# Attention kernel, first stage: layer norm and q, k, v projections rebuilt with split products, a pipeline of chunks and early loads

## The reference

```
xn = layernorm(x)                                         # over the 256 channels
result = x + attention(xn) * silu(ffn(xn))
# attention(x):
q, k, v = x @ Wq.T + bq, x @ Wk.T + bk, x @ Wv.T + bv      # x is 4096 x 256; 16 heads of 16
x*cos + rotate_half(x)*sin                                # on q and k; rotate_half pairs even and odd channels
scores = q @ k.T / sqrt(16), causal; weights = softmax(scores); out = weights @ v
```

## Time and profile before

| | us |
|---|---|
| median of three runs | 3974.87 (3970.74 to 3975.3) |
| the profiled execution | 3964.55 |
| its span, first to last instruction | 3962.8 |
| TensorE busy | 3379.4 |
| DVE busy | 2420.3 |
| ScalarE busy | 1698.9 |
| GpSimd busy | 668.5 |

### The profile page before, as it was taken

The page is one execution under the profiler, slowest core; times in us unless marked ns, Lnnn a source line. Parts: engine busy times, 40 slices in busy tenths (PEclk is TensorE's granted clock), DMA queues, the critical chain, the costliest instruction groups (busy, mean ns, idle before and its releaser), DMA issues. The chain is left out here.

```text
span 3962.8 us, 77279 instructions
## 1 busy us (share of the span) xinstructions
PE 3379.4 (85%) x32524; PEld 2009.1 (51%) x32524; DVE 2420.3 (61%) x3345; ACT 1698.9 (43%) x3090; POOL 668.5 (17%) x464
## 2 busy tenths in 40 slices
PE   5836999999999999999975899985996899995895
PEld 2412333333444333333344676764775677774784
DVE  4325888778767888767524556553553565562554
ACT  1202666677765777777622332321222332321221
POOL 4410000000000000000002333320222433330221
PEclk9966999999999999999878999997998999998897
DMA  5484000020003000000012000000001000000003
GB/s 169 137 146 96 18 9 10 10 62 17 10 26 86 18 17 10 9 4 7 7 57 85 17 18 18 18 7 28 0 0 34 23 18 12 18 12 28 0 0 127
DMA packets 82083, 137.61 MB, mean 35 GB/s; under 512 B 11024, under 2 KB 41872, under 8 KB 80800
## 3 DMA queue, kind: packets, MB, share of 16 engines
q1 hardware_dynamic: 75376, 122.64, 10.9%
q10 hardware_dynamic: 6400, 10.49, 1.0%
HBM read 90.04 MB, written 42.53 MB: 33 GB/s over the span
## 5 line engine op out<-in xcount | busy, mean ns | idle before, releaser
L509 DVE TENSOR_REDUCE mp<-ps_m 128x2 f32<-128x1024 f32 (+3 forms) x1152 | 1287.3, 1135 | 400.3 <-PE ps_m L557 278.8
L485 ACT ACTIVATE probs<-ps_s 128x512 f32<-128x512 f32 (+3 forms) x2304 | 1166.3, 560 | 632.3 <-PE ps_s L592 339.3
L606 PE MATMUL ps_o<-probs,vst 128*32 128x256 f32 (+3 forms) x9216 | 723.9, 386 | 3.1 <-ACT o_sb L474 2.0
L585 PE MATMUL ps_s<-qst,kst 64*128 64x512 f32 (+3 forms) x2304 | 596.0, 496 | 59.5 <-DMA qst<-mrow 50.8
L557 PE MATMUL ps_m<-kst,qst 64*128 64x512 f32 (+3 forms) x2304 | 487.5, 415 | 74.9 <-DMA qst<-null_rows 62.4
L585 PEld LDWEIGHTS ps_s<-qst,kst 64*128 64x128 f32 x2304 | 235.5, 190 | 524.6 <-ACT probs L485 432.6
L606 PEld LDWEIGHTS ps_o<-probs,vst 128*32 128x32 f32 x9216 | 187.9, 110 | 333.7 <-issue 215.4
L462 POOL TENSOR_TENSOR msplit<-negm,mzero 128x16 fp32r<-128x16 f32 x32 | 7.1, 223 | 1759.9 <-DVE negm L515 1759.9
L557 PEld LDWEIGHTS ps_m<-kst,qst 64*128 64x128 f32 x2304 | 229.8, 192 | 132.8 <-issue 69.0
L1205 DVE SCALAR_TENSOR_TENSOR a_t<-a_BP,a_sc,a_tab 128x256 f32<-128x256 f32 x384 | 166.6, 475 | 188.0 <-ACT a_sq L905 187.4
L884 ACT ACTIVATE a_PT<-a_SU 128x1024 f32<-128x1024 f32 (+1 forms) x128 | 122.5, 1009 | 333.0 <-PE a_SU L1002 333.0
(11 more groups left out here) (160 smaller groups left out, 5176.1 us busy)
## 6 DMA issues: line engine op xcount, KB each, us to landing
a_tab<-in_rope SPq DMA_DIRECT2D x32, 512.0 KB
q_parts<-pparts SPq DMA_DIRECT2D x32, 256.0 KB
k_parts<-pparts SPq DMA_DIRECT2D x32, 256.0 KB
v_aug<-pvsb SPq DMA_DIRECT2D x32, 256.0 KB
qst<-q_parts SPq DMA_DIRECT2D x64, 128.0 KB, 2.7
o_raw<-o_sb SPq DMA_DIRECT2D x32, 256.0 KB, 2.1
X<-in_x SPq DMA_DIRECT2D x8, 512.0 KB, 15.7
kst<-k_parts SPq DMA_DIRECT2D x32, 128.0 KB, 5.7
```

The costliest lines, as they stand in the source:

```text
L485: act.activation(probs[:, s % PR, h, off:C], sslots[n % SR][:, off:C], ACT.Exp, scale=float(D) ** -0.5).then_inc(exp_done, 1)
L509: dve.tensor_reduce(mp[b % 2][:, h:h + 2, cc:cc + 1], slot[:, :, 0:width], AX.X, ALU.max).then_inc(max_read, 1)
L585: last = pe.matmul(sslots[n % SR][:, off:C], kst[g % 2][rows, hp, i * P:(i + 1) * P], qst[q_slot(b)][rows, hp, off:C], start=True, stop=True)
L606: last = pe.matmul(ps_o[32 * h:32 * h + VW, lo:hi], vst[g % 2][:, i, h * VW:(h + 1) * VW], probs[:, s % PR, h, lo:hi], start=(i == 0 and h ...
```

## The change

**Split products.** Weights and normalized x are each split into a rounded part and its rest (`w_h`, `w_l`, `xh`, `xl`), and each projection is three products of such parts (`product3`) instead of one fp32 product. The weights of q and k have their even channels first and their odd channels behind, so that no swapped copy is projected: the rotation takes even times cos less odd times sin, and even times sin plus odd times cos. A group is now all of q or all of k (`u`), with even and odd halves (`s`).

**Pipeline.** Each engine works on several chunks by turns: DVE measures chunk c+3, ACT normalizes chunk c+2, PE transposes chunk c+1 between q's and k's products of chunk c. Tables come chunk by chunk. One of the four low parts of a chunk moves to DVE (`low_last`), three stay on POOL. Each of q and k has one buffer of parts. Normalization moves to ACT.

**Values in SBUF.** V stays in one tile `vall`, with rows of 17 and read 32 wide, filled by ACT; its bias comes from a product with ones. `v_aug` and `vst` are gone.

**Null rows.** They are memsets of the whole kst and qst tiles by POOL instead of DMAs; the ones rows come from a small tile. kst1 is zeroed on POOL ahead of its work on block 2, and SP's loads of group 1 wait for that.

**Early loads.** Blocks 0 to 3 of keys and queries of group 0 are loaded in the projection stage, each one chunk after it was written (`preload`).

The diff, cut: removed lines are left out, since they stand above in the kernel before, and so are declarations and the head of each engine's program.

```diff
-def layer_norm_and_project(nc, ctx0, X, x, w_qkv, b_cols, b_v, cos, sin, ident, k_parts, q_parts, v_aug, ones, nulls):
+def project(nc, X, kst, qst, vall, consts, x, w_qkv, b_cols, b_v, cos, sin, ident, identb, mask_k, mask_q, k_parts, q_parts):
...
+            def preload(c):
+                for u in range(2):
+                    sp.wait_ge(parts_out[u], 16 * 4 * (c + 1))
+                load_k_block(sp, kst[0], k_parts, 0, c, pre_in)
+                load_q_block(sp, qst[c], q_parts, 0, c, pre_in)
...
+            for c in range(NC):
+                if c + 4 < NC:
+                    load_x(c + 4)
+                if c == 0:
+                    sp.wait_ge(qst_null, NPRE)
+                for u in range(2):
+                    if u == 1 and c + 2 < NC:
+                        sp.wait_ge(rope_done, 8 * (c + 1))
+                        load_cs(c + 2)
+                    sp.wait_ge(lo_pool, 3 * c + 2 + u)
+                    if u == 1:
+                        sp.wait_ge(lo_dve, c + 1)
+                    dst = (q_parts, k_parts)[u]
+                    for n in range(4):
+                        sp.dma_start(dst[:, n // 2, 8 * (n % 2):8 * (n % 2) + 8, c * C:(c + 1) * C],
+                                     parts[:, u, n, :].bitcast(F32)).then_inc(parts_out[u], 16)
+                    if u == 0 and 0 < c <= NPRE:
+                        preload(c - 1)
...
+        @block.gpsimd
...
+            pool.memset(kst[0][:, 0, :].bitcast(F32), 0.0).then_inc(kst_null, 1)
+            inverse(0)
+            pool.memset(kst[0][:, 1, :].bitcast(F32), 0.0).then_inc(kst_null, 1)
+            inverse(1)
+            for i in range(NPRE):
+                pool.memset(qst[i][:, :, :].bitcast(F32), 0.0).then_inc(qst_null, 1)
+            for c in range(NC):
+                if c + 2 < NC:
+                    inverse(c + 2)
+                for u in range(2):
+                    k = 2 * c + u
+                    for s in range(2):
+                        pool.wait_ge(rope_done, 4 * k + 3 + s)
+                        if c > 0:
+                            pool.wait_ge(hi_done, 2 * (k - 2) + s + 1)
+                            if u == 1 and s == 1:
+                                pool.wait_ge(lo_dve, c)
+                            else:
+                                pool.wait_ge(lo_pool, 3 * (c - 1) + 2 * u + s + 1)
+                        pool.tensor_tensor(rot[:, u, s, :], t[:, u, 2 * s, :], t[:, u, 2 * s + 1, :],
+                                           (ALU.subtract, ALU.add)[s]).then_inc(rot_done, 1)
+                    for s in range(2 - u):
+                        pool.wait_ge(rot_done, 2 * k + s + 1)
+                        pool.wait_ge(hi_done, 2 * k + s + 1)
+                        pool.tensor_tensor(parts[:, u, 2 + s, :], rot[:, u, s, :], parts[:, u, s, :].bitcast(F32), ALU.subtract
+                                           ).then_inc(lo_pool, 1)
+        @block.scalar
...
+            def round_part(c, u, s):
+                act.wait_ge(rot_done, 2 * (2 * c + u) + s + 1)
+                if c > 0 and s == 0:
+                    act.wait_ge(parts_out[u], 16 * 4 * c)
+                act.activation(parts[:, u, s, :], rot[:, u, s, :], ACT.Copy).then_inc(hi_done, 1)
...
+            for c in range(NC):
+                for s in range(2):
+                    if c + 1 < NC:
+                        high(c + 1, s)
+                    round_part(c, 0, s)
+                if c + 2 < NC:
+                    normalize(c + 2)
+                for s in range(2):
+                    round_part(c, 1, s)
...
+        @block.tensor
...
+            for c in range(NC):
+                b = c % 2
+                for u in range(2):
+                    for s in range(2):
+                        if c > 0:
+                            pe.wait_ge(rope_done, 8 * (c - 1) + 4 * u + 2 * s + 2)
+                        col = u * E + s * P
+                        for e in range(EC):
+                            if u == 0 and s == 0:
+                                pe.wait_ge(xl_done, c * EC + e + 1)
+                            last = product3(pe, ps_p[u][:, s, :], w_h[:, e, col:col + P], w_l[:, e, col:col + P],
+                                            xh[:, b, e, :], xl[:, b, e, :], e == 0, e == EC - 1)
+                        last.then_inc(p_done, 1)
+                    if u == 0 and c + 1 < NC:
+                        turn(c + 1)
...
+        @block.vector
...
+            def low_last(c):
+                dve.wait_ge(rot_done, 4 * c + 4)
+                dve.wait_ge(hi_done, 4 * c + 4)
+                dve.tensor_tensor(parts[:, 1, 3, :], rot[:, 1, 1, :], parts[:, 1, 1, :].bitcast(F32), ALU.subtract
+                                  ).then_inc(lo_dve, 1)
...
+            for c in range(NC):
+                rope(c, 0)
+                if c > 0:
+                    low_last(c - 1)
+                if c + 1 < NC:
+                    low(c + 1)
+                if c + 2 < NC:
+                    center(c + 2)
+                rope(c, 1)
+                if c + 3 < NC:
+                    measure(c + 3)
+            low_last(NC - 1)
...
+def load_k_block(eng, kst, k_parts, g, j, done):
+    cols = slice(j * C, (j + 1) * C)
+    kh = k_parts[g * GH:(g + 1) * GH, :, :, cols].rearrange("(p x) t d n -> x (t d) p n", x=2)
+    for x in range(2):
+        eng.dma_start(kst[ROWS * x:ROWS * x + 2 * D, :, cols].bitcast(F32), kh[x]).then_inc(done, 16)
+        eng.dma_start(kst[ROWS * x + 2 * D:ROWS * x + KQ, :, cols].bitcast(F32), kh[x, 0:D]).then_inc(done, 16)
+def load_q_block(eng, qst, q_parts, g, j, done):
+    qh = q_parts[g * GH:(g + 1) * GH, :, :, j * C:(j + 1) * C].rearrange("(p x) t d n -> x (t d) p n", x=2)
+    for x in range(2):
+        eng.dma_start(qst[ROWS * x:ROWS * x + D, :, :].bitcast(F32), qh[x, 0:D]).then_inc(done, 16)
+        eng.dma_start(qst[ROWS * x + D:ROWS * x + KQ, :, :].bitcast(F32), qh[x]).then_inc(done, 16)
...
+            load_k_block(eng, kst[g % 2], k_parts, g, j, k_in[g % 2][j])
+                load_q_block(sp, qst[q_slot(b)], q_parts, g, j, q_in[q_slot(b)])
+            for b in range(NPRE, QR):
+                load_k(sp, 0, b)
+                sp.wait_ge(q_null, b - NPRE + 1)
+            sp.wait_ge(one_set, 1)
+            sp.wait_ge(k_null, 1)
+            for x in range(2):
+                sp.dma_start(kst[1][ROWS * x + KQ:ROWS * x + KM, :, :].rearrange("a p (b n) -> a (p b) n", n=P).bitcast(F32),
+                             one[:, :]).then_inc(one_in, 16)
...
+            for i in range(NPRE, QR):
+                pool.memset(qst[i][:, :, :].bitcast(F32), 0.0).then_inc(q_null, 1)
+            pool.memset(one[:, :], 1.0).then_inc(one_set, 1)
+                if b == 2:
+                    pool.memset(kst[1][:, :, :].bitcast(F32), 0.0).then_inc(k_null, 1)
...
-                    last = pe.matmul(ps_o[32 * h:32 * h + VW, lo:hi], vst[g % 2][:, i, h * VW:(h + 1) * VW],
+                    last = pe.matmul(ps_o[32 * h:32 * h + VW, lo:hi], vall[:, i, (g * GH + h) * DV:(g * GH + h) * DV + VW],
...
+    halves = np.concatenate([np.arange(0, E, 2), np.arange(1, E, 2)])
+    arr["w_qkv"] = rows(np.concatenate([wq[halves].T, wk[halves].T, wv.T], axis=1))
```

More of the change, by code:

```diff
@@ L33 @@
 VW = 32
+VALL = (H - 1) * DV + VW
+NPRE = 4
 LH, LD = 8, 64
@@ L89, in layer_norm_and_project @@
         rstd = sb("prstd", [P, NT])
[L90 to L98, removed]
+        nmr = sb("pnmr", [P, NT])
+        xh, xl = (sb(f"px{i}", [P, 2, EC, C], F32R) for i in "hl")
@@ L140, in chunk @@
[L140 to L163, removed]
+            def load_cs(c):
+                sp.dma_start(cs[:, c % 2, 0, :], cos[:, c * C:(c + 1) * C]).then_inc(cs_in[c % 2], 16)
+                sp.dma_start(cs[:, c % 2, 1, :], sin[:, c * C:(c + 1) * C]).then_inc(cs_in[c % 2], 16)
@@ L208, in _, with normalize, high @@
-            repeat(act, NC, chunk)
+            def normalize(c):
+                act.wait_ge(nmr_done, c + 1)
+                for a in range(TPC):
+                    n = c * TPC + a
+                    act.activation(X[:, n, :], X[:, n, :], ACT.Identity, scale=rstd[:, n:n + 1], bias=nmr[:, n:n + 1]
+                                   ).then_inc(xn_done, 1)
+            def high(c, e):
+                act.wait_ge(t_done, c * EC + e + 1)
+                if c >= 2:
+                    act.wait_ge(v_done, 2 * (c - 1))
+                act.activation(xh[:, c % 2, e, :], ps_t[:, e, :], ACT.Copy).then_inc(xh_done, 1)
@@ L231, in chunk @@
[L231 to L237 removed]
+                        last = product3(pe, ps_v[:, a, :], xh[:, b, e, tok], xl[:, b, e, tok], w_h[:, e, 2 * E:WC],
+                                        w_l[:, e, 2 * E:WC], False, e == EC - 1)
@@ L337, in global_attention @@
         QR, MR, SR, PR = 8, 2, 3, 3
-        kst = [sb(f"kst{i}", [P, PAIRS, S], F32R) for i in range(2)]
-        qst = [sb(f"qst{i}", [P, PAIRS, C], F32R) for i in range(QR)]
```

(5 more changed lines are left out.)

350 lines of the change are left out of this document (168 added, 182 removed).

## The result

The changed kernel takes **3797.95 us** (median of four executions, 3784.53 to 3808.00), the kernel before 3972.8 in the same session; the ratio is 0.9564, interval [0.9543, 0.9584]. The forecast was 3820, range 3800 to 3850: the direction is right, the median lies 22 us under the forecast and 2 us under the range. A second session gave 3800.14 (five executions).

A forecast was written before the change was run, and what follows sets the result against it. Until 340 us projection and barrier (236), loading (42.4) and first product to first score (61.6) bound it, not arithmetic. First product at 125 instead of 278 (-153) gives 3811.6; 10.3 more for the median, about 3820, range 3800 to 3850.

The forecast's parts named there:

- Head, about 20: Start of the projection: first rotation at about 20 us, where before even the products began only at 38.
- One chunk, 11 us: Projection: a chunk's turn takes 11 us, followed through GpSimd's work, with GpSimd, TensorE and DVE nearly level.
- DMA in the stage, 9: Projection: parts, tables and early block loads landing late in chunks 1 to 4 cost 9 us, between 0 and 18.
- rival 1: Projection: DMA fully hidden, the turn stays 11 throughout, 9 us less, 3811; chance 0.20.
- Tail, 18: End of the projection: the last chunk's sums and parts, issues, landing and barrier take 18 us.
- Start of attention, 62 from first product to first score: Attention start: SP's first mrow waits behind GpSimd's memset and group 1's loads; 62 us against 61.6, nothing gained or lost.
- Rival 2: Projection: SP becomes the loop, four turns of 17 to 18 us, costing 25 instead of 9, 3836; chance 0.20.
- Rival 3: Attention start: mrow later still as memset or queue takes longer, +10 to 18 us, 3834; chance 0.08.
- Rival 4: Projection: DVE and GpSimd block each other, at most 1.6 us in all, or +10 with whole waits, 3830; chance 0.07.
- Rival 5: Projection: TensorE stays at 1.2 GHz, a chunk takes 18.4 us, the kernel 3870; chance 0.05.
- Rival 6: Attention: V's rows of 17 slow the 9216 weight loads, the gain is gone or the kernel slower, up to 4125; chance 0.03.
- The rest, 3625 us, the change does not reorder: From the first score to the end: the time stays 3625 us, as before the change.

The follow-up runs named there:

- again: The changed kernel run once more with no edit; median 3800.14 us.
- bv_first: Changed kernel with GpSimd's four memsets of the q buffers waiting until DVE has scaled the low part of V's bias; 3807.09 us.
- short_low: Changed kernel with one of GpSimd's seven large operations a chunk, a low part of q, made for 64 of 512 columns; early turns 10.65 and 11.24 us.
- one_fp32: Changed kernel with one fp32 product of the high halves for each three split products, also in local layers and MLP; 3939.92 us, early turns 11.66.
- late_loads: Changed kernel with blocks 0 to 3 loaded at the start of the attention stage instead of during the projection; 3804.3 us.
- mrow_first: Changed kernel with SP issuing group 1's ones rows and 32 loads behind the mrow transfers of blocks 0 and 1, not ahead; 3781.56 us.

## Why the prediction was right, and where it failed

- **What bounds the first 340 us: right.** The three pieces named are the ones that changed, or stayed, as the result shows.
- **Head, about 20: 22.26** (21.42 in again). The working adds up to 19.1; the missing step is DVE's scaling of the bias beside GpSimd's memsets, 2.3 to 3.2 too long, and bv_first brings 19.07.
- **One chunk, 11 us: 11.1** while the parts land in time, but not GpSimd alone, as I followed it: GpSimd and TensorE are level (short_low, one_fp32).
- **DMA in the stage, 9 (bounds 0 and 18): 4.5** by the two long turns (13.7 and 13.0 against 11.1; I had expected four), 6.3 by late_loads. So it was neither hidden (rival 1) nor as dear as I took it. I took 217 GB/s for the reads from a stretch that also held V's loads. The agreement with the Trainium skill (SBUF — State Buffer, Door 1: The DMA port swizzle) was only half read: that section gives a transfer to 16 partitions four ports and about 109 GB/s, so by it the reads of a chunk, two thirds at 218 GB/s and one third at 109, would take an estimated 4.8 us and not 3.6. The mixed traffic of a turn was held to neither, 305 GB/s at a share of 0.96.
- **Tail, 18:** 19.5 from the last chunk's first rotation (near 102.7) to the opening.
- **Start of attention, 62 from first product to first score: 61.0.** mrow_first shows that the wait was the one named.
- **Rival 2** (SP as the loop) did not come: no turn of 17. **Rival 3** no. **Rival 4** in small: DVE's last low part takes 0.68 alone and up to 1.34 beside GpSimd, where I gave 0.2 a turn for GpSimd's side; DVE was busy 9.4 to 9.8 us of a turn, so it had room for this. The dearer form of it stood in the head, where I had put nothing for it. **Rival 5** no: granted 1.00 in the turns. **Rival 6** no: 386 ns for a product with V in both kernels.
- **The step that failed is "The rest, 3625 us, the change does not reorder", with "ScalarE's v loads later in the stage are covered likewise": a term put at nothing.** The attention behind the first score got 12 us shorter, 1691 to 1679 in the mean of the profiles, past the change of 10 that the prediction itself named as a sign of being wrong. Some 7 of the 12 are TensorE's waits for exponentials. The 3622.4 against 3623.1 of the profiled pair looked like a hit by luck.
- **The second part of the miss is the saving ahead of the first score.** I took 153 from one execution of before, whose first score came at 339.67; two more had it at 345.13 and 345.56, and the changed kernel has it at 182.54 and 183.77, so 162 is typical. Of these 9 us, 6 are that one early execution and 3 are too much in my sum. With the 12 this is 21; less 1.9 that I rounded off it is 19 of the 22, and the rest is within the spread of the executions: 162 and 12 off a median of 3973 give 3799, where 3797.95 and 3800.14 were measured.
- **The 10.3 for the step to the median** only set the 153 against the median of before instead of one execution, which is sound, since it is the saving that carries over. That the profiled execution, at 3808.00, came so near the 3811.6 of the sum was luck: it was 10 over its own median. The range, which ended at 3800, left no room for a saving above the sum.

## What to carry to other kernels

A profiled execution is one draw. Take the saving from several executions of the kernel before, set it against the median, and widen the range on both sides. Compare stage by stage, since two equal totals can hide differences that cancel. Before a stage is called untouched, go through the queues in it: here the loads on SP and ScalarE had changed, and the stage called untouched got 12 us shorter. Behind a stage whose engines are level, undoing one improvement moves little, because another wait stands right behind it; what counts is the work that is gone. And a queue that issues both urgent and early transfers is best read for what stands ahead of the urgent one: here a reordering of SP's transfers was worth 26 us.

## What the hardware showed unasked

A TENSOR_SCALAR of 256 elements a partition took 3.55 us (2.65 in again) on DVE beside GpSimd memsets, ten times its 0.35 alone. A tiny operation (four elements a partition, 0.15 us where GpSimd rests) took 1.14 in one_fp32 while GpSimd worked:

```profile
38.71 1.14 DVE L330 SCALAR_TENSOR_TENSOR pnmr<-pmv,prstd 128x4 f32<-128x4 f32 x1
```

And the same program, with TensorE over 96% busy in the 80 us before, once kept 2.4 GHz and once fell to 1.2 GHz for most of 20 us at the same place.
